# New orders of the pieces on four engines, and y multiplied between two rows of gathers

## What is computed

```
x = ln(x + ssd(x))        # A: projection, two chunked state-space sums, rms norm, gate silu(z), W_out
x = ln(x + ffn(x))        # B1, B2: silu(gate) * up, down, 704 hidden, integer weights
x = ln(x + (x + u*silu(g) @ w_out))   # B3 to B6: q, k, v; y = sigmoid(q) * cumsum(exp(k)*v) / cumsum(exp(k)); 1024 hidden
x = ln(x + moe(x))        # C, D: top 4 of 16 experts, 448 hidden
```

## Time and profile before

| | |
|---|---|
| median of 3 runs | 1944.17 us (1938.99 to 1944.36) |
| profiled execution | 1946.5 us, span 1944.7 us |
| mean granted TensorE clock | 0.954 |
| TensorE matmul busy | 1704.5 us (88%) |
| VectorE | 1306.3 us (67%) |
| GpSimd | 868.5 us (45%) |
| ScalarE | 735.3 us (38%) |

### The profile page before, as it was taken

How to read it: one execution, slowest core, us unless ns; L and a number is a source line. 1 busy time by engine, 2 the same in 40 slices (tenths; PEclk the granted TensorE clock), 3 DMA queues, 4 the chain that set the end, 5 groups by cost and what they waited for, 6 DMA issues and landing times. The chain is left out here.

```text
span 1944.7 us, 34693 instructions
## 1 busy us (share of the span) xinstructions
PE 1704.5 (88%) x8516; PEld 1210.0 (62%) x8517; DVE 1306.3 (67%) x3087; ACT 735.3 (38%) x1400; POOL 868.5 (45%) x823
## 2 busy tenths in 40 slices
PE   4489999999999999999999998863999999999970
PEld 2267768667677677677686675651555566666550
DVE  4688888878888878878888787431444444444435
ACT  3244354354354344443553542221222233333223
POOL 2033353343433433533533433123666677777654
PEclk8799999999999999999999999886999999999995
DMA  4633133142142241331331421645999999999987
GB/s 155 209 89 111 47 115 100 46 125 81 54 135 67 68 135 41 94 110 46 115 99 46 125 78 53 263 148 172 159 161 161 162 172 173 173 171 169 171 134 259
DMA packets 369400, 242.70 MB, mean 125 GB/s; under 512 B 250624, under 2 KB 348224, under 8 KB 368960
## 3 DMA queue, kind: packets, MB, share of 16 engines
q1 hardware_dynamic: 303552, 170.12, 33.1%
q0 software_dynamic: 40704, 67.40, 18.9%
q10 hardware_dynamic: 25088, 4.50, 1.3%
HBM read 121.23 MB, written 68.78 MB: 98 GB/s over the span
## 5 line engine op out<-in xcount | busy, mean ns | idle before, releaser
L1698 PE MATMUL pu<-w_all,xh 128*128 x1728 | 363.6, 357 | 53.3 <-DMA xh<-xin 35.8
L1698 PEld LDWEIGHTS pu<-w_all,xh 128*128 128x128 bf16 x1728 | 168.4, 98 | 206.8 <-issue 90.5
L1829 POOL DMA_INDIRECT sums_dram<-yo,meta_in x144 | 229.0, 1591 | 132.8 <-issue 66.9
L1781 DVE TENSOR_TENSOR hid<-pu,gate 128x448 f32<-128x448 f32 x144 | 90.0, 625 | 250.0 <-PE pu L1698 134.3
L838 PE MATMUL pb<-x1T,w_sw 128*128 128x256 f32 x1024 | 232.5, 383 | 0.7 <-ACT x1T L957 0.7
L838 PEld LDWEIGHTS pb<-x1T,w_sw 128*128 128x128 f32 x1024 | 195.3, 192 | 50.4 <-issue 18.1
L1713 PE MATMUL py<-w_all,hh 128*128 x1584 | 197.1, 273 | 1.6 <-DMA hh<-hs 1.6
L1713 PEld LDWEIGHTS py<-w_all,hh 128*128 128x128 bf16 x1584 | 155.3, 98 | 43.2 <-issue 2.5
L1816 POOL DMA_INDIRECT xin<-x_dram,meta_in x144 | 142.4, 989 | 66.7 <-issue 46.2
L776 PE MATMUL pb<-x1T,w_gu 128*128 128x256 f32 x704 | 166.6, 387 | 1.9 <-ACT x1T L957 0.7
L653 PE MATMUL pa<-w_in,xT 128*128 128x512 f32 (+1 forms) x384 | 159.5, 554 | 9.2 <-DMA bc_bias<-in_bc_bias 8.3
(11 more groups left out here) (249 smaller groups left out, 2934.5 us busy)
## 6 DMA issues: line engine op xcount, KB each, us to landing
w_stage<-in_w_ug SPq DMA_DIRECT2D x64, 224.0 KB, 2.9
split_ug<-w_parts SPq DMA_DIRECT2D x64, 224.0 KB, 2.9
w_all<-split_ug SPq DMA_DIRECT2D x16, 896.0 KB, 9.3
xg_dram<-xg SPq DMA_DIRECT2D x16, 512.0 KB, 3.1
w_stage<-in_w_dn SPq DMA_DIRECT2D x32, 256.0 KB, 2.9
split_dn<-w_parts SPq DMA_DIRECT2D x32, 256.0 KB, 2.5
w_all<-split_dn SPq DMA_DIRECT2D x16, 512.0 KB, 10.3
rows<-sums_dram SPq DMA_DIRECT2D x32, 256.0 KB, 5.6
```

The source lines that it names most:

```text
L1698: last = mm(pu[:, 2 * b + w, 0:EH], xh[:, m % XS, DC * xp + c, :], w_ug[:, bass.ds(e, 1), wp, c, w * EH:(w + 1) * EH], start=n == 0, stop= ...
L1829: nc.gpsimd.indirect_dma_start(out=sums_dram[m % 2], out_offset=bass.IndirectOffsetOnAxis(ap=meta[:, m, 0:1], axis=0), in_=yo[:, m % XS, : ...
```

## The change

Only the strings in `ORDER` change, except SyncE's. No instruction is added or taken away.

```diff
 ORDER = {
     "SP": ("CE C7 A0 N0 A2 WL.0 WL.1 AR C9 WL.2 WL.3 WL.4 WL.5 CF"),
-    "PE": ("C7 A2 C7L F3.0 F3.1 B1T A2L B1.0 C8 B1.1 A3 B1.2 B1.3 B1.4 A3L B1.5 B2.0 B2.1 A4.0 A4.1 G1+ B3T A4.2 B3.0 "
-            "B3.1 B3V A4.3 B4.0 G2.0+ B4.1 A4.4 G2.1+ B5T A4.5 B5.0 B5.1 A4.6 B5.2 B5.3 B5.4 A4.7 B5.5 B5.6 B5.7 B6.0 "
+    "PE": ("C7 A2 C7L F3.0 F3.1 B1T C8 A2L B1.0 A3 B1.1 B1.2 B1.3 B1.4 A3L B1.5 B2.0 B2.1 A4.0 G1+ A4.1 B3T A4.2 B3.0 "
+            "B3.1 B3V A4.3 A4.4 B4.0 G2.0+ B4.1 G2.1+ B5T A4.5 B5.0 B5.1 A4.6 B5.2 B5.3 A4.7 B5.4 B5.5 B5.6 B5.7 B6.0 "
             "A5.0 B6.1 A5.1 A6.0 A6.1"),
-    "ACT": ("A2 WH.0 C7 C7L A2S F3 WH.1 B1T C8 A2L B1.0 B1.1 B1.2 A3 WH.2 B1.3 B1.4 A3L B1.5 G1+ B3T WH.3 G2+ B3.0 B3.1 "
-            "B3L.0 B3L.1 G3+ B5T B5.0 B5.1 B5.2 B5.3 B5.4 B5.5 B5.6 WH.4 A5 B5.7 A5L WH.5 G4+"),
-    "POOL": ("C7 A6- A2 AX.0 AX.1 A2L B2 B3.0 B3.1 D8+ G1+ A5 B6"),
-    "DVE": ("A2 A6L- A2G WL.0 C7L C7H A2R C8 B1.0 B1.1 C9 A2L B1.2 AV B1.3 B1.4 A3L B1.5 AU.0 AU.1 WL.1 WL.2 AU.2 AU.3 B2 "
-            "A4.0 B2L AY.0 A4.1 G1+ B2M AU.4 AU.5 AY.1 A4.2 G1B+ B3.0 B3.1 A4.3 B4E B4.0 B4.1 G2+ AU.6 AY.2 AU.7 A4.4 "
-            "AY.3 B5.0 AY.4 B5.1 A4.5 A4.6 B5.2 G4.0+ B5.3 AY.5 B5.4 AY.6 B5.5 A4.7 AY.7 B5.6 WL.3 G4.1+ B5.7 A5 WL.4 "
+    "ACT": ("C7 A2 C7L A2S F3 C8 B1T A2L B1.0 WH.0 B1.1 A3 B1.2 WH.1 B1.3 B1.4 A3L B1.5 WH.2 G1+ B3T G2+ B3.0 B3.1 B3L.0 "
+            "B3L.1 WH.3 B5T B5.0 B5.1 B5.2 WH.4 B5.3 B5.4 B5.5 G4+ B5.6 A5 B5.7 WH.5 G3+ A5L"),
+    "POOL": ("C7 A6- A2 AX.0 A2L AX.1 B2 B3.0 B3.1 G1+ D8+ A5 B6"),
+    "DVE": ("A2 C7L A6L- C7H A2G A2R C8 B1.0 C9 B1.1 WL.0 A2L B1.2 AV B1.3 B1.4 A3L B1.5 WL.1 AU.0 AU.1 AU.2 WL.2 AU.3 B2 "
+            "A4.0 B2L AU.4 G1+ AY.0 AU.5 A4.1 A4.2 G1B+ AY.1 B2M B3.0 A4.3 B3.1 B4E B4.0 B4.1 AY.2 G2+ WL.3 A4.4 AU.6 "
+            "AY.3 B5.0 AU.7 B5.1 A4.5 AY.4 B5.2 G4.0+ A4.6 B5.3 AY.5 B5.4 AY.6 B5.5 A4.7 AY.7 B5.6 G4.1+ B5.7 A5 WL.4 "
             "G4.2+ B6 WL.5 B6L A6"),
 }
```

## The result

The changed kernel takes 1912.84 us (median of 4 runs, 1906.69 to 1916.05), the kernel before 1942.02 us beside it (4 runs, 1938.99 to 1944.36): a ratio of 0.9846 with a 95% interval of 0.9824 to 0.9867. 1916 had been forecast. The profiled execution took 1916.05 us, with a span of 1914.2, against 1944.7 before.

What follows compares the result with a forecast made beforehand. TensorE, busy 1704.5 of 1944.7 us, was taken as the bound, so only its gaps and the start could be won: -21 - 1.7 - 2 - 4 + 1 = -27.7 from the median 1944.17, giving 1916 us; 8-in-10 range 1904 to 1945.

Steps and rivals of the forecast that it cites:

- The main term: TensorE's idle time before the down projection of the first feed-forward part (B2, L790) goes: -21 us.
- The gap before B2: TensorE's 23.8 us of waits for hidden tiles at L790 go once y splits the gathers: -21, bounds 0 to -28.
- (a): Before B2: B1.4's result reaches ScalarE's silu 1.4 us late, during the row of seven gathers; part of 23.8 us.
- (b): Before B2: `masked` collides with GpSimd's y, taking 3.42 us instead of 1.17, and h_tail waits; part of 23.8 us.
- C8 and A4.4: TensorE: count matmuls fill the gap before A2L, -1.7 us; A4.4 fills the gap before B4.0, -2 us.
- x1T behind an exponential: ScalarE: table load and ez now precede the x1T copy, still in time for B1.0: 0, at worst +1.3 us a round.
- Rival 3: Table load before x1T delays B1.0 each round, +19.5 us; chance within 0.13 (large term won) and 0.12 (not won).
- The start: First full round: earlier store of weight piece 1 and load_rest, less ScalarE's added work: -4 us, bounds 0 to -7.
- The end: Rounds without layer A: table load before x1T and C7L before A6L lengthen the latency chain: +1 us, 0 to +3.
- The moves priced at 0: G1+, G3+, G4+, the WL and WH weight pieces, AU.4 and the A3/B1.1 swap: hidden or neutral, 0 us.
- Rival 1: TensorE's late results stay and B2 keeps its 23.8 us: -6.7 us, about 1938 us; chance 0.17.

Runs made afterwards that it cites:

- The kernel before with y between and held back: Kernel before with two edits, y after the fourth gather and waiting for VectorE's scales: 1913.4 us, again 1912.0 us.
- the long pause: Changed kernel, y behind all seven gathers, GpSimd waiting for the copy of cb_own and multiplying one small tile between gathers four and five: 1950.7 us.
- the short one: Changed kernel, y behind all seven gathers, GpSimd waiting for the scales and multiplying one small tile between gathers four and five: 1946.8 us.

## Why the prediction was right, and where its sizes were off

By the rounds from the first full A2L (99.40 us before, 97.28 now) to the last (1158.58 and 1130.23) the difference in span, 30.5 us, splits into 26.2 in the rounds, 2.1 ahead of them and about 2.1 behind. That the forecast of 1916 came so near is in part luck. The main term was 9 us too small; the collision, the clock and the second round (together +7) were not in the sum at all, the start gave 2 us less than forecast and the end 3 us more, and these errors nearly cancel.

- **The gap before B2, forecast -21, bounds 0 to -28.** Both mechanisms were named rightly, and both went. The sign and the place were right; the size was -30, outside the bound. The kernel before with y between and held back has rounds of 73.06 against 75.22: 14 x 2.16 = 30. The bound added 0.3 us a round to the 23.8 us of the list, but what is added belongs to each gap, and the list has 23 gaps (11 + 5 + 7). Without a gap B2 begins 0.17 us before the modelled end of B1.5 (557.07 against 557.24 above), and its first ten matmuls take 2.32 us instead of 2.42; by an estimate from these, 23.8 + 23 x 0.27 = 30. The 0.2 to 0.5 us a round kept for `masked` and AU.3 was not used. Mechanisms (a) and (b) cost the same in the first trace: `masked` ended at +16.5 in a round of either kind, and both took 75.2 us.
- **What was missed: y and L1283, +4.9.** The prediction checked y against `masked` and not against the wide instructions ahead of it. In the undisturbed round y begins 0.84 us behind the end of L1283. With the first gather 1.3 us earlier it begins while L1283 runs, and three rounds paid 1.63 us each. One more clock dip than before (3 against 2, 1.6 to 2 us each) takes about 1 back, and the second round another 1 (its excess over an undisturbed round went from 2.3 to 3.3). -30 - 3 + 4.9 + 1 + 1 gives the 26.2.
- **C8 and A4.4, forecast -1.7 and -2.** Together about -2.4 to -3: 14 x 0.17 by the kernel with both edits, 14 x 0.21 by the undisturbed round before the wait was added. All other moves of the three orders are in this number too; no run parts them. L820 waits 0.2 us instead of 5.4, and 0.24 us a round came back before B5T, as the step said; the wait for zs fell from 4.7 to 2.5.
- **x1T behind an exponential, forecast 0.** ez is issued 1.29 us after its table load at 544.14, x1T copied from 545.55, and B1.0 starts at 546.23 without a wait. Rival 3 falls by this. The Trainium skill ("ScalarE: Activation LUTs", What ACT_TABLE_LOAD costs) adds about 1.38 us of drain to each load; this trace disagrees again.
```profile
544.14 1.28 ACT L1004 ACT_TABLE_LOAD   x1
545.43 0.21 ACT L1004 ACTIVATE ez<-ez 128x8 f32<-128x8 f32 x1
545.55 0.58 ACT L957 ACTIVATE x1T<-pb 128x512 f32<-128x512 f32 x1
```
- **The start, forecast -4, came -2.1.** SyncE's store of piece 1 moved from 47.80 to 39.62, as forecast, and ScalarE's long wait ends 4.4 us earlier instead of the 7 taken; then a table load and xs (2.4 us) stand ahead of the squares. So the transfers gave less than the store did. In eleven more traces the first full A2L lies at 98.1 to 99.5 us (mean 98.5, 4 traces) with the old orders and at 94.8 to 98.5 (mean 96.8, 7 traces) with the new ones, 1.7 us apart.
```profile
39.62 0.55 SPq L598 DMA_DIRECT2D split_ug<-w_parts  x1
```
```profile
77.20 0.63 ACT L1013 ACTIVATE w_parts<-w_stage 128x512 bf16<-128x512 f32 x1 [23.49 <-DMA w_stage<-in_w_dn]
```
- **The end, forecast +1, came about -2.1**, 1.7 of it from the last A2L to L881, among TensorE's first work behind the layers. Behind the last A2L the list of waits has 2.1 us at L790 for hT before and none now, and 3.0 us at L820 before and 2.1 now; that these are the 1.7 us is not shown.
- **The moves priced at 0** held with ScalarE's and VectorE's new orders together. With ScalarE's order alone put back the kernel is 3% slower than before, and some 5% slower than the changed kernel, so cover shared by two engines should have been priced as a pair.

The gathers and y came within half a us of their steps (first at +5.65, as its step had +6, y at +10.9, as it had +11.3). Rival 1, that the late results stay, falls: they went with y between the gathers and with the long pause, and came back with y behind them and with the short one. What it rested on stands: the round at 176.92 us of the kernel before has the same seven gathers and no late result, and no run says why.

## What to carry to other kernels

When a wide GpSimd instruction moves, check it against every wide VectorE instruction within the time that the engines can run ahead of each other, not only against the one that it used to hit; an order keeps them apart only as long as no engine runs ahead, a wait on what must be over first does it in every round. Here the wait cost nothing that the time could show. Before laying out all orders anew, try the one move that carries the mechanism, with such a wait: here two edits gave what the new orders of four engines gave. A single engine's order is not a unit of change, as the loads of another engine may be tied to it.

## What the runs showed of the hardware

- A VectorE instruction that starts shortly before GpSimd's 128x1024 multiply does not keep its place. L1283 started 0.20 us ahead of y and ended 0.96 us after y's end (3.14 us, 1.08 alone); L1524 started 0.32 us ahead and took 2.79 instead of 0.62 us. The Trainium skill ("SBUF — State Buffer", SBUF: two separate sides) gives the shared pair of ports to whichever starts first, for its whole instruction, of a VectorE instruction with two inputs in SBUF and a GpSimd instruction that reads SBUF. The blocking is in the traces; that the first keeps the ports is not, by the starts that the profile records: against this multiply the VectorE instruction lost each time, though it had started first.
- It also goes the other way. A gather that is under way when VectorE's L1263 starts on `decay` takes 1.2 to 1.7 us in the steady rounds instead of 0.95, and ends within 0.05 us of it: the fourth at 555.09 as L1263 does, and the fifth of the kernel before at 563.98, with L1263 at 563.97.
- In a row of seven gathers with breaks of 0.30 to 0.42 us TensorE's results reach their consumers late in most rounds, from the fifth gather to 1.0 us and more behind the seventh (1.4 us in the earlier trace rows, 2.2 us at 495.46 above, 2.1 us at 565.57). One instruction of 0.19 us between the fourth and the fifth did not cure it, 2.2 to 2.5 us without gathers did, and then the results came in time during the later gathers too.
- TensorE's granted clock falls from 2.4 to 1.2 GHz for 3.4 us now and then: not at all to eight times in 14 rounds of the kernels here (the one with ScalarE's old order left out), after waits of 2 us or more, but also with no gap over 0.4 us in the 4 us ahead. It costs 1.6 to 2 us a time and, where the engines that ran ahead then collide, as much again in the next round.
